# A decoder layer on one core: delta times h on GpSimd, the softmax's division behind the mix, six joins, the skip product by ScalarE, new queue orders

## The chip, the cores and the metric

One core of a Trainium2 chip runs the kernel. The time is the device time in microseconds of one execution, from the first instruction to the last. Only TensorE, VectorE (DVE in the profile), ScalarE (ACT), GpSimd (POOL) and the DMA queue that SyncE (SP) feeds take part.

## What is computed

128 sequences of 64 tokens with 128 features pass through one layer of three sublayers, each added to its input and followed by a layer norm: a Mamba block, a cross attention with 16 heads of 8, and a mixture of 8 experts (top 2) with a shared one. Cut to what the change touches:

```python
conv = silu(causal_conv4(hidden))                 # h in the kernel
delta = softplus(ts @ dt_w + dt_b)
new = exp(A * d_t) * state + d_t * B_t * h_t      # 16 states for each of 256 channels
y = einsum('bin,bn->bi', new, C_t) + D * h_t      # D * h is the skip product
out = (y * silu(gate)) @ out_w
...
scores = einsum('bhqd,bhkd->bhqk', qh, kh) / sqrt(8)
attn = softmax(scores)                            # exp and a division by the row's sum
out = einsum('bhqk,bhkd->bhqd', attn, vh) @ Wo.T + bo
```

## The kernel before, in words

The tokens are cut into 16 chunks of 8 sequences (T = 512 tokens), everything in fp32 but the B rows. A chunk passes through five stages: head (RMS norm, input projection), front (convolution, delta), scan (the 16 states), back (output of the block, attention, routing, the experts' first half) and tail (rest of the experts, last norm). In turn t, chunk t is in scan, t+1 in front, t+2 in head, t-1 in back and t-2 in tail, so up to five chunks are in flight. What each engine does in a turn, and in what order, is written out by hand as a list of steps for each of the four engines and SyncE, in three versions: FIRST_TEXT for the turns up to 1, ORDER_TEXT for the middle, LAST_TEXT from turn 15. An engine runs its list strictly in order and waits on semaphores; where the list begins a turn is only a cut in a cycle. Four PSUM banks form a ring (IN_RING) that TensorE's steps take in the order of its own list.

The steps that matter here:

- **delta** (VectorE, L1049) adds the two parts of the softplus; behind it in the same step VectorE multiplies delta with h into u (L1052), 128 x 1024. **drive** n (L1008) multiplies u with the B row, which TensorE has spread over the partitions (B_row, L609), into PSUM. **decay** (ScalarE, L766) is exp(A delta), one step per state and half. **scan** n (L1018) runs the recurrence over all tokens. **prod** n (GpSimd, L1149) multiplies the state with the C row, which SyncE has fetched (step C, L578) into one of four slots.
- **y_sum** (TensorE, L627) adds prod n into p_y through the identity matrix, one matmul for each of the two halves. For n in JOINED GpSimd first adds prod n-1 to prod n (L1154), and n-1 has no matmuls. **y_d** (L618) is the first matmul into p_y, diag(D) times h, and clears the bank. **gated** (VectorE, L1059) multiplies p_y with the gate.
- The attention of a chunk goes sequence by sequence, i = 0 to 7: **score** (TensorE, L697, with VectorE's row maximum, L1068), **exp** (ScalarE, L898, 8 activations that also give the sums den), **sum** (VectorE, L1072, reciprocal of den), **scale** (GpSimd, L1202, ex times the reciprocal), **turn** (TensorE, L702, four transposes, which wait for scale; ScalarE copies them out, L907), **mix** (TensorE, L710; copied out into aT, L913), and after four sequences **aout** (L716, L717), the output projection.
- **k** (GpSimd, L1193, L1196) and **km** (ScalarE, L887) build the masked keys from kT; **add_bo** is L1185. **x1T** is copied at L862 and the first convolution tap is L812. In the expert part **up_g** and **up_u** (TensorE, L728) feed ScalarE's tanh (L937) and copies (L945), VectorE (L1118, L1123) and GpSimd's gu and cw (L1214, L1223), which reads routing weights fetched by **cw_in** (L589).

```python
if i >= C_SLOTS or c.m >= 1:                               # step C, SyncE
    sp.wait_ge(prod_ready.sem, prod_ready.at(c.m, i - C_SLOTS))
...
pe.wait_ge(scale_ready.sem, scale_ready.at(c.m, i))        # step turn, TensorE
```

## Time and profile before

| | |
|---|---|
| median of 3 runs | 1906.67 us (1904.21 to 1908.64) |
| the profiled execution: its own time | 1910.89 us |
| its span, first to last instruction | 1909.1 us |
| mean granted TensorE clock | 0.962 of full |
| matmul records, TensorE | 7035 |
| DMA | 140.50 MB, 74 GB/s on average |

The page gives busy time per engine and groups the instructions by line. Further views cut the span into stretches, list who waited for whom, and follow the chain that ended last. An fp32 matmul shows as two matmul records. Mean durations of ScalarE and TensorE overlap with the next instruction's, so the pitch, where it matters, is read from a run of equal instructions.

### The profile page before, as it was taken

To read this page: it belongs to the slowest core of one execution; us is meant where nothing else is said; L and a number is where in the kernel's file an instruction comes from. 1 tells how busy PE (TensorE), PEld (TensorE's weight loads), DVE (VectorE), ACT (ScalarE), POOL (GpSimd) and SP (SyncE) were. 2 spreads that over 40 slices of the span, in tenths; PEclk is the share of its full clock that TensorE was granted. 3 is DMA by queue.
4 is the path that set the end of the run, shared out by engine and by line. 5 is a ranking of instruction groups with operands and counts; after the bars stand their busy time and mean duration, and the time that the engine had idled before them with its cause. 6 is when DMAs were issued, how large, how long until landed. Compare 5 with 4: busy or idle time off the path is not lost. (4 is left out here: it accounts for less than half of the span.)

```text
span 1909.1 us, 25699 instructions
## 1 busy us (share of the span) xinstructions
PE 1684.5 (88%) x7035; PEld 964.7 (51%) x7138; DVE 1539.7 (81%) x1891; ACT 1398.8 (73%) x4370; POOL 1529.5 (80%) x1284
## 2 busy tenths in 40 slices
PE   3679989999898999999899899989989999998976
PEld 1235454655545465554646455464645546465544
DVE  4988988888888888889888888888888888878422
ACT  5478787786977768787777869777787977867361
POOL 0578888888888888888888898888889888898734
PEclk7789999999999999999999999999999999999988
DMA  3212221313222131222213122221312222121102
GB/s 103 80 47 73 88 75 61 95 40 96 82 84 78 52 91 54 89 75 96 81 52 92 53 90 82 89 79 52 90 55 89 76 82 83 66 85 55 63 7 66
DMA packets 125918, 140.50 MB, mean 74 GB/s; under 512 B 44048, under 2 KB 69456, under 8 KB 125776
## 3 DMA queue, kind: packets, MB, share of 16 engines
q1 hardware_dynamic: 125776, 138.86, 23.8%
q8 instruction: 58, 0.95, 0.2%
q14 instruction: 84, 0.69, 0.1%
HBM read 133.84 MB, written 4.98 MB: 73 GB/s over the span
## 5 line engine op out<-in xcount | busy, mean ns | idle before, releaser
L1149 POOL TENSOR_TENSOR prod<-state,c_rep 128x1024 f32<-128x1024 f32 x256 | 605.4, 2368 | 39.8 <-PE p_y L627 23.7
L1018 DVE TENSOR_TENSOR_SCAN state<-decay,p_drive 128x1024 f32<-128x1024 f32 x256 | 584.6, 2284 | 28.5 <-ACT decay L766 15.2
L627 PE MATMUL p_y<-prod,ident 128*128 128x512 f32 x768 | 391.4, 609 | 10.2 <-POOL prod L1149 5.7
L766 ACT ACTIVATE decay<-delta,a_neg 128x504 f32<-128x504 f32 x512 | 359.3, 725 | 43.4 <-DVE state L1018 42.0
L1008 DVE TENSOR_TENSOR p_drive<-u,p_drive 128x1024 f32<-128x1024 f32 x256 | 312.2, 1220 | 66.4 <-PE p_drive L609 36.2
L898 ACT ACTIVATE ex<-p_ring,nmax 128x64 f32<-128x64 f32 x1024 | 310.1, 369 | 19.8 <-DVE nmax L1068 19.4
L898 ACT ACTIVATION_READ_ACCUMULATOR ex<-p_ring,nmax 128x1 f32 x1024 | 255.4, 262 | 0.0
L728 PE MATMUL p_ring<-x2T,wg 128*128 128x512 f32 x416 | 226.8, 650 | 13.2 <-ACT gh L823 12.3
L1202 POOL TENSOR_TENSOR ex<-ex,rden 128x512 f32<-128x512 f32 x128 | 144.2, 1127 | 94.1 <-DVE rden L1072 94.1
L728 PE MATMUL p_ring<-x2T,wu 128*128 128x512 f32 x416 | 208.9, 603 | 7.5 <-DVE km L1118 6.5
L627 PEld LDWEIGHTS p_y<-prod,ident 128*128 128x128 f32 x768 | 139.6, 194 | 143.8 <-issue 116.9
L1223 POOL TENSOR_TENSOR km<-km,cwr 128x512 f32<-128x512 f32 x128 | 179.6, 1413 | 21.5 <-DMA cwr<-cw_rows 20.3
L937 ACT ACTIVATE gt<-p_ring 128x512 f32<-128x512 f32 x208 | 123.0, 593 | 88.7 <-PE p_ring L728 88.1
L922 ACT ACTIVATE x<-p_ring,shift,rstd 128x128 f32<-128x128 f32 x192 | 78.2, 463 | 148.7 <-POOL shift L1174 147.9
L697 PE MATMUL p_ring<-km,qs 128*128 128x512 f32 x256 | 135.4, 622 | 25.6 <-ACT x L922 12.7
L1154 POOL TENSOR_TENSOR prod<-prod 128x1024 f32<-128x1024 f32 x64 | 151.6, 2368 | 5.0
L710 PE MATMUL p_ring<-exT,vm 128*128 128x128 f32 x1024 | 140.6, 280 | 10.1 <-ACT exT L907 8.3
L728 PEld LDWEIGHTS p_ring<-x2T,wg 128*128 128x128 f32 x416 | 82.3, 205 | 126.2 <-issue 82.9
L710 PEld LDWEIGHTS p_ring<-exT,vm 128*128 128x128 f32 x1024 | 125.0, 191 | 33.1 <-issue 12.0
L744 PE MATMUL p_ring<-wd,km 128*128 128x128 f32 x1024 | 127.9, 279 | 6.9 <-POOL acts_more L1223 6.8
L1214 POOL TENSOR_TENSOR km<-km,us 128x512 f32<-128x512 f32 x80 | 102.6, 1285 | 38.4 <-ACT us L945 37.0
L992 DVE BATCH_NORM_STATS2 stats<-p_ring 128x6 f32<-128x128 f32 x192 | 47.1, 287 | 105.4 <-PE p_ring L744 78.9
(139 smaller groups left out, 3080.1 us busy)
## 6 DMA issues: line engine op xcount, KB each, us to landing
c_rep<-c_rows SPq DMA_DIRECT2D x256, 256.0 KB, 3.6
cwr<-cw_rows SPq DMA_DIRECT2D x64, 256.0 KB, 3.2
ctxT<-in_ctx_t SPq DMA_DIRECT2D x32, 256.0 KB, 5.6
cwr<-cw_rows SPq DMA_DIRECT2D x32, 224.0 KB, 3.1
cwr<-cw_rows SPq DMA_DIRECT2D x32, 192.0 KB, 2.7
cwr<-cw_rows SPq DMA_DIRECT2D x32, 160.0 KB, 2.9
xf<-in_x SPq DMA_DIRECT2D x16, 256.0 KB, 5.9
xb<-in_x SPq DMA_DIRECT2D x16, 256.0 KB, 4.8
```

Source lines behind the costliest of these rows:

```text
L627: pe.matmul(p_y[1 - first][:], ident[:], prod[:, slot_of(c, n), 1 - first, :], start=False, stop=n == STATE - 1).then_inc(prod_used.sem, 1)
L697: mm = pe.matmul(p[:], qs[:, i, :, :].rearrange("p s q -> p (s q)"), km[:, i, :, :].rearrange("p a k -> p (a k)"), start=True, stop=True)
L710: mm = pe.matmul(p[:, 0:128], vm[:, i, q, :], exT[:, q, :], start=q == 0, stop=q == QUADS - 1)
L728: mm = pe.matmul(p[:], (wg if name == "up_g" else wu)[:, i, :], x2T[:], start=True, stop=True)
L766: act.activation(decay[:, n % 2, j, :].rearrange("p (b t) -> p b t", t=SEQ)[:, :, 1:], delta[:, c.parity, j, :].rearrange("p (b t) -> p b ...
L898: e = act.activation(ex[:, i % 2, a, :], p[:, a * SEQ:(a + 1) * SEQ], ACT.Exp, bias=nmax[:, i % 2, a:a + 1], accum_out=den[:, i % 2, a:a + 1])
L1008: dve.tensor_tensor(p_drive[:], u[:, c.parity, :, :], p_b.unsqueeze(1).to_broadcast([128, HALVES, T]), ALU.mult).then_inc(drive_ready.sem, 1)
L1018: dve.tensor_tensor_scan(state[:, slot_of(c, n), :, :].rearrange("p j t -> p (j t)"), decay[:, n % 2, :, :].rearrange("p j t -> p (j t)"), ...
L1149: pool.tensor_tensor(mine, state[:, slot_of(c, n), :, :], c_rep[:, n % C_SLOTS, :].unsqueeze(1).to_broadcast([128, HALVES, T]), ALU.mult). ...
L1154: pool.tensor_tensor(mine, mine, prod[:, slot_of(c, n - 1), :, :], ALU.add).then_inc(join_ready.sem, 1)
L1202: pool.tensor_tensor(ex[:, i % 2, :, :], ex[:, i % 2, :, :], by_group(rden[:, i % 2, :]).to_broadcast([128, PAIRS, SEQ]), ALU.mult).then_i ...
L1223: pool.tensor_tensor(acts[i], acts[i], cwr[:, slot, :], ALU.mult).then_inc(act_ready.sem, 1)
```

## The change

- JOINED has six members where it had four.
- The product u leaves VectorE's delta step and becomes a step of GpSimd, in the stage front. delta, drive0 and scan0 stand in front as well.
- The skip product: y_d is a step of ScalarE, which writes D times h straight into p_y; the matmuls of y_sum add to that. diag_d goes. Two matmuls at the start write p_y once.
- Softmax: scale goes; turn takes the undivided exponentials. sum takes the reciprocals of four sequences at once. ScalarE's new step spread repeats each reciprocal over the 8 features of its head, into kT's space; TensorE's new step rden transposes that by the identity into a bank of the ring; VectorE's new step share multiplies four sequences of aT by it. aout waits for share.
- All lists of steps are new. Shown are those of GpSimd and SyncE for the middle turns and the end of ScalarE's, which continues with scan.decay6 and back.v0; VectorE's list has "tail.up_g12 back.gated0 back.gated1". In it ScalarE's spread0 stands between decay19 and exp6, y_d1 between decay11 and q0, spread1 behind turn7.

```diff
--- before.py
+++ after.py
@@
-JOINED = (1, 9, 11, 13)
+SIDE = CHUNK_B // 2
+JOINED = (1, 3, 7, 9, 11, 13)
@@ ORDER_TEXT @@
     "act": (
...
+        "head.hid0 head.tap0 back.up_g11 front.gate_tanh1 back.up_g12 back.up_u10 front.decay4 "
+        "head.hid1 scan.k0 head.gate0 head.tap1 front.decay5 front.y_d0"),
...
     "pool": (
-        "tail.cw10 back.stats0 back.stats1 scan.prod0 tail.stats4 scan.prod1 back.k0 tail.stats5 "
-        "scan.prod2 back.scale0 scan.prod3 back.scale1 back.scale2 scan.prod4 scan.prod5 back.add_bo0 "
-        "back.scale3 scan.prod6 back.scale4 scan.prod7 scan.add_out_b0 back.scale5 scan.prod8 "
-        "back.scale6 back.stats2 back.scale7 scan.prod9 scan.prod10 back.stats3 scan.prod11 "
-        "scan.prod12 back.r_rank0 back.gu1 scan.prod13 back.cw0 back.cw1 back.gu2 head.mean0 back.gu4 "
-        "back.cw2 back.gu5 scan.prod14 back.cw3 back.cw4 scan.prod15 back.cw5 back.cw6 back.gu7 "
-        "back.gu8 back.cw7 back.cw8 back.gu10 back.cw9"),
+        "tail.cw7 tail.gu8 tail.cw8 tail.cw9 tail.gu10 tail.cw10 back.stats0 back.stats1 scan.prod0 "
+        "tail.stats4 scan.prod1 back.k0 tail.stats5 scan.prod2 scan.prod3 scan.prod4 scan.prod5 "
+        "back.add_bo0 scan.prod6 scan.prod7 scan.prod8 back.stats2 scan.prod9 scan.prod10 "
+        "scan.add_out_b0 back.stats3 scan.prod11 back.r_rank0 scan.prod12 back.gu1 scan.prod13 "
+        "back.gu2 back.cw0 head.mean0 back.cw1 front.u0 back.gu4 back.cw2 back.cw3 scan.prod14 "
+        "back.gu5 back.cw4 scan.prod15 back.cw5 back.gu7 back.cw6"),
     "sp": (
-        "back.C7 back.C10 scan.C_out0 back.C13 back.C11 back.C12 tail.cw_out0 tail.cw_in0 back.C14 "
-        "tail.cw_in1 back.C15 tail.cw_in2 tail.cw_in3 tail.cw_in4 scan.C0 tail.cw_in5 tail.cw_in6 "
-        "tail.cw_in7 scan.C1 scan.C3 tail.cw_in8 tail.cw_in9 tail.cw_in10 scan.C5 scan.C2 scan.C4 "
-        "scan.C6 scan.xb_in0 head.x_in0 tail.out0 scan.C9 scan.C8"),
+        "tail.cw_in5 scan.C2 tail.cw_in6 tail.cw_in7 tail.cw_in8 tail.cw_in9 scan.C3 tail.cw_in10 "
+        "scan.C5 scan.C4 scan.C9 scan.C7 scan.C8 scan.C6 scan.C11 head.x_in0 scan.C10 tail.out0 "
+        "scan.C13 front.C_out0 scan.xb_in0 scan.C12 front.C0 scan.C14 back.cw_out0 back.cw_in0 "
+        "back.cw_in1 back.cw_in2 scan.C15 back.cw_in3 front.C1 back.cw_in4"),
...
         ga = kT[:]
+        spread = kT[:].rearrange("p (b c) -> p b c", c=128)
...
             pe.matmul(p_b[:, 0:D], column(V_BV).to_broadcast([128, 128]), wattn[:, 3, :],
                       start=True, stop=True).then_inc(bv_ready.sem, 1)
+            for j in range(HALVES):
+                pe.matmul(p_y[j][:], ident[:], wattn[:].rearrange("d w o -> d (w o)"),
+                          start=True, stop=True).then_inc(y_open.sem, 1)
             def spread_b(c, n):
...
-            def skip_d(c, i):
-
-                j = 1 - i
-                pe.wait_ge(h_ready.sem, h_ready.at(c.m, j))
-                if c.m >= 1:
-                    pe.wait_ge(yg_ready.sem, yg_ready.at(c.m - 1, i))
-                pe.matmul(p_y[j][:], diag_d[:, j, :], h[:, c.parity, j, :], start=True, stop=False)
-
             def sum_n(c, k):
                 n, first = divmod(k, HALVES)
+                if sum_index(k) < HALVES:
+                    pe.wait_ge(skip_ready.sem, skip_ready.at(c.m, first))
                 if n in JOINED:
                     pe.wait_ge(join_ready.sem, join_ready.at(c.m, JOINED.index(n)))
                 else:
                     pe.wait_ge(prod_ready.sem, prod_ready.at(c.m, n))
                 pe.matmul(p_y[1 - first][:], ident[:], prod[:, slot_of(c, n), 1 - first, :],
-                          start=False, stop=n == STATE - 1).then_inc(prod_used.sem, 1)
+                          start=False, stop=n == STATE - 1, skip_group_check=True
+                          ).then_inc(prod_used.sem, 1)
             def step(name, i, c):
                 if name == "less":
...
                 elif name == "turn":
-                    pe.wait_ge(scale_ready.sem, scale_ready.at(c.m, i))
+                    emptied(pe, "score", i, c.m)
                     for q in range(QUADS):
                         mm = pe.transpose(p[:, q * 128:(q + 1) * 128],
...
+                elif name == "rden":
+                    pe.wait_ge(spread_ready.sem, spread_ready.at(c.m, i))
+                    for b in range(SIDE):
+                        mm = pe.matmul(p[:, b * 128:(b + 1) * 128], spread[:, b, :], ident[:], start=True, stop=True)
                 elif name == "aout":
                     pe.wait_ge(x1b_ready.sem, x1b_ready.at(c.m))
-                    emptied(pe, "mix", (i + 1) * CHUNK_B // 2 - 1, c.m)
+                    emptied(pe, "rden", i, c.m)
                     for g in range(2):
                         pe.matmul(p[:, g * D:(g + 1) * D], ident[:], x1b[:, 2 * i + g, :], start=True, stop=False)
                         mm = pe.matmul(p[:, g * D:(g + 1) * D],
...
                     act.wait_ge(max_ready.sem, max_ready.at(c.m, i))
+                    if c.m >= 1:
+                        act.wait_ge(rden_ready.sem, rden_ready.at(c.m - 1, i // SIDE))
                     for a in range(PAIRS):
                         e = act.activation(ex[:, i % 2, a, :], p[:, a * SEQ:(a + 1) * SEQ], ACT.Exp,
-                                           bias=nmax[:, i % 2, a:a + 1], accum_out=den[:, i % 2, a:a + 1])
+                                           bias=nmax[:, i % 2, a:a + 1], accum_out=den[:, i, a:a + 1])
                     e.then_inc(free("score", i, c.m), 1)
                 elif name == "turn":
                     p = filled(act, name, i, c.m)
@@ -906,6 +906,18 @@
                         filled(act, "mix", CHUNK_B - 1, c.m - 1)
                     act.activation(exT[:].rearrange("p a q -> p (a q)"), p[:],
                                    ACT.Copy).then_inc(free(name, i, c.m), 1)
+                elif name == "spread":
+                    act.wait_ge(rden_ready.sem, rden_ready.at(c.m, i))
+                    if i == 0:
+                        act.wait_ge(km_ready.sem, km_ready.at(c.m))
+                        act.wait_ge(km_more.sem, km_more.at(c.m))
+                    else:
+                        filled(act, "rden", 0, c.m)
+                    mine = rden[:, SIDE * i:SIDE * (i + 1), :].unsqueeze(3).to_broadcast([128, SIDE, PAIRS, HEAD_D])
+                    for s in range(2):
+                        a = act.activation(spread[:, :, 64 * s:64 * s + 64].rearrange("p b (a d) -> p b a d", d=HEAD_D),
+                                           mine, ACT.Copy)
+                    a.then_inc(spread_ready.sem, 1)
                 elif name == "mix":
                     p = filled(act, name, i, c.m)
                     for s in range(2):
...
                 elif name == "decay":
                     decays(c, i)
+                elif name == "y_d":
+                    j = 1 - i
+                    act.wait_ge(h_ready.sem, h_ready.at(c.m, j))
+                    if c.m >= 1:
+                        act.wait_ge(yg_ready.sem, yg_ready.at(c.m - 1, i))
+                    else:
+                        act.wait_ge(y_open.sem, y_open.at(0, j))
+                    act.activation(p_y[j][:], h[:, par, j, :], ACT.Copy, scale=column(V_D + j)
+                                   ).then_inc(skip_ready.sem, 1)
...
                     dve.tensor_tensor(delta[:, par, :, :], delta[:, par, :, :], sp_a[:], ALU.add
                                       ).then_inc(delta_ready.sem, 1)
-                    dve.wait_ge(delta_ready.sem, delta_ready.at(c.m))
-                    dve.tensor_tensor(u[:, par, :, :], delta[:, par, :, :], h[:, par, :, :], ALU.mult
-                                      ).then_inc(u_ready.sem, 1)
                 elif name == "gated":
                     j = 1 - i
...
                 elif name == "sum":
-                    emptied(dve, "score", i, c.m)
-                    dve.reciprocal(rden[:, i % 2, :], den[:, i % 2, :]).then_inc(rden_ready.sem, 1)
+                    mine = slice(SIDE * i, SIDE * i + SIDE)
+                    emptied(dve, "score", SIDE * i + SIDE - 1, c.m)
+                    if c.m >= 1:
+                        dve.wait_ge(spread_ready.sem, spread_ready.at(c.m - 1, i))
+                    dve.reciprocal(rden[:, mine, :].rearrange("p b a -> p (b a)"),
+                                   den[:, mine, :].rearrange("p b a -> p (b a)")).then_inc(rden_ready.sem, 1)
+                elif name == "share":
+                    p = filled(dve, "rden", i, c.m)
+                    emptied(dve, "mix", SIDE * i + SIDE - 1, c.m)
+                    mine = slice(SIDE * SEQ * i, SIDE * SEQ * (i + 1))
+                    for s in range(2):
+                        r = slice(64 * s, 64 * s + 64)
+                        a3 = aT[r, mine].rearrange("p (b q) -> p b q", q=SEQ)
+                        d = dve.tensor_tensor(a3, a3, p[r, :].rearrange("p (b s q) -> p b s q", b=SIDE, s=2)[:, :, s, :],
+                                              ALU.mult)
+                    d.then_inc(free("rden", i, c.m), 1)
                 elif name == "route":
                     p = filled(dve, name, i, c.m)
                     logits = p[:, 0:GROUPS * EXPERTS].rearrange("p (g e) -> p g e", e=EXPERTS)
...
                                                masks[:, a:a + 1], 0.0, ALU.mult, ALU.add)
                     g.then_inc(km_ready.sem, 1)
-                elif name == "scale":
-                    emptied(pool, "score", i, c.m)
-                    pool.wait_ge(rden_ready.sem, rden_ready.at(c.m, i))
-                    pool.tensor_tensor(ex[:, i % 2, :, :], ex[:, i % 2, :, :],
-                                       by_group(rden[:, i % 2, :]).to_broadcast([128, PAIRS, SEQ]),
-                                       ALU.mult).then_inc(scale_ready.sem, 1)
                 elif name == "r_rank":
                     pool.wait_ge(route_v.sem, route_v.at(c.m, 4))
                     pool.tensor_tensor(r_eq, r_eq, tri[:].unsqueeze(1).to_broadcast(
                         [128, GROUPS, EXPERTS, EXPERTS]), ALU.mult).then_inc(route_g.sem, 1)
                     pool.wait_ge(route_g.sem, route_g.at(c.m, 0))
                     pool.tensor_tensor(r_gt, r_gt, r_eq, ALU.add).then_inc(route_g.sem, 1)
+                elif name == "u":
+                    pool.wait_ge(h_ready.sem, h_ready.at(c.m, 1))
+                    pool.wait_ge(delta_ready.sem, delta_ready.at(c.m))
```

## Rows read from the trace of the kernel before

**Rows 1.** The page: busy time, share and instructions of each engine
```profile
PE 1684.5 (88%) x7035; PEld 964.7 (51%) x7138; DVE 1539.7 (81%) x1891; ACT 1398.8 (73%) x4370; POOL 1529.5 (80%) x1284
```

**Rows 2.** The delta step: shortest, median, longest in ns, first and last start
```profile
L1049 DVE TENSOR_TENSOR delta<-delta,sp_a x16: 1224/1271/1972, 40.2 to 1662.4; 128x1024 f32<-128x1024 f32 x16
```

**Rows 3.** Busy time by stretch: the lead-in and ten periods
```profile
core 0: us, PE busy (x) PEld busy (x) DVE busy (x) ACT busy (x) POOL busy (x), PEclk, DMA share, GB/s
0.00:208.45 208.45, 141.48 (x394) 63.40 (x400) 161.10 (x164) 137.76 (x361) 118.07 (x80) 0.83 0.23 70
...
321.04:1437.65 1116.61, 1024.65 (x4388) 593.43 (x4459) 960.60 (x1170) 869.21 (x2731) 957.85 (x801) 0.99 0.25 77
```

**Rows 4.** The chain that ended last, in time: start, us, what
```profile
1775.68 4.29 PE p_ring L728 x10
...
1800.70 2.90 PE p_ring L744 x26
```

**Rows 5.** Groups of TensorE: busy and mean | idle before
```profile
L627 PE MATMUL p_y<-prod,ident 128*128 128x512 f32 x768 | 391.4, 609 | 10.2 <-POOL prod L1149 5.7 <-POOL prod L1154 4.3
...
L618 PE MATMUL p_y<-h,diag_d 128*128 128x512 f32 x64 | 32.4, 621 | 0.1
```

**Rows 6.** Groups of GpSimd
```profile
L1149 POOL TENSOR_TENSOR prod<-state,c_rep 128x1024 f32<-128x1024 f32 x256 | 605.4, 2368 | 39.8 <-PE p_y L627 23.7 <-DVE state L1018 11.9 <-DMA c_rep<-c_rows 4.2
...
L1202 POOL TENSOR_TENSOR ex<-ex,rden 128x512 f32<-128x512 f32 x128 | 144.2, 1127 | 94.1 <-DVE rden L1072 94.1
```

**Rows 7.** Waits in ten periods, 321.04 to 1437.65: us, times, longest
```profile
POOL ex L1202 <- DVE rden L1072: 54.0, 40, 2.3
...
PE p_ring L702 <- POOL ex L1202: 5.3, 20, 0.3
```

**Rows 8.** VectorE: u's shortest, median, longest in ns, then groups
```profile
L1052 DVE TENSOR_TENSOR u<-delta,h x16: 1225/2170/2178, 41.4 to 1663.7; 128x1024 f32<-128x1024 f32 x16
...
L1123 DVE TENSOR_TENSOR km<-kT,p_ring 128x512 f32<-128x512 f32 x48 | 32.5, 677 | 1.6 <-PE p_ring L728 1.2
...
L1052 DVE TENSOR_TENSOR u<-delta,h 128x1024 f32<-128x1024 f32 x16 | 31.9, 1994 | 0.6
L1072 DVE RECIPROCAL rden<-den 128x8 f32<-128x8 f32 x128 | 24.4, 191 | 9.7 <-ACT ex L898 9.7
...
L1091 DVE TENSOR_TENSOR x1T<-r_prob 128x256 f32<-128x256 f32 x16 | 6.8, 424 | 0.6
```

**Rows 9.** Groups of ScalarE
```profile
L937 ACT ACTIVATE gt<-p_ring 128x512 f32<-128x512 f32 x208 | 123.0, 593 | 88.7 <-PE p_ring L728 88.1 <-DVE km L1118 0.4
...
L913 ACT ACTIVATE aT<-p_ring 64x64 f32<-64x64 f32 x256 | 58.0, 226 | 8.3 <-PE p_ring L710 6.6
L887 ACT ACTIVATE km<-kT,masks 128x512 f32<-128x512 f32 x48 | 31.1, 712 | 29.8 <-PE p_ring L744 29.8
...
L812 ACT ACTIVATE zc<-hpad,halfv 128x512 f32<-128x512 f32 x32 | 25.8, 807 | 0.1
...
L862 ACT ACTIVATE x1T<-p_ring 128x256 f32<-128x256 f32 x32 | 11.9, 380 | 1.6 <-PE p_ring L678 1.6
```

**Rows 10.** Busy time by stretch: the attention part of one period
```profile
820.50:838.50 18.00, 15.93 (x59) 8.20 (x60) 16.67 (x19) 17.88 (x96) 15.42 (x10) 1.00 0.43 110
```

**Rows 11.** The C rows: issue ns, waits, landing us, and add_bo
```profile
L578 SPq DMA_DIRECT2D c_rep<-c_rows x256: 319/426/1450, 30.9 to 1763.8; - x128
...
  DMA c_rep<-c_rows: 4.2, 1
...
DMA to landing us min/median/max: 3.0/3.6/6.1
...
L1185 POOL TENSOR_TENSOR x1b<-x,rowb 128x512 f32<-128x512 f32 x16 | 20.4, 1274 | 0.0
```

**Rows 12.** VectorE in order of time: two successive scans
```profile
831.46 2.29 DVE L1018 TENSOR_TENSOR_SCAN state<-decay,p_drive 128x1024 f32<-128x1024 f32 x1
...
836.02 2.29 DVE L1018 TENSOR_TENSOR_SCAN state<-decay,p_drive 128x1024 f32<-128x1024 f32 x1
```

62 lines of the change are left out of this document (48 added, 14 removed), and 260 rows, old and new, of tables (FIRST_TEXT, LAST_TEXT, ORDER_TEXT).

## The prediction

> **What bounds the kernel now.** I read the page's first part, then cut the span at the delta step, which comes once per chunk, then the waits, and last the long groups of each engine. The page names TensorE the busiest engine [rows 1]. There are 16 delta steps, the last at 1662.4 us [rows 2]; the third is at 208.45, so 13 periods take 1454.0 us, 111.8 us for one chunk. In ten whole periods from 321.04 to 1437.65 TensorE is busy for 1024.65 of 1116.61 us, VectorE for 960.60, GpSimd for 957.85 and ScalarE for 869.21 [rows 3]. Per period that is TensorE 102.5 busy and 9.2 idle, VectorE 96.1, GpSimd 95.8, ScalarE 86.9. The granted clock there is 0.99, the 2.4 GHz level, so there is nothing to win from the clock in the middle. What is idle on TensorE is split into many short gaps, and in long runs of 512-column matmuls there is no gap at all. I therefore take TensorE's instruction stream as the bound, with VectorE and GpSimd 6 us behind. The reader should see in [rows 1] how close the four engines stand: whatever is taken from TensorE alone pays in full only until the next one is full.
>
> **TensorE, part by part.** An fp32 matmul is two records. Ten records of 512 columns take 4.29 us, so one such matmul costs 0.86 us; 26 records of 128 columns take 2.90 us, so a small one costs 0.223 [rows 4]. Two more joins drop two states from the sum into p_y, each with two matmuls: 4 x 0.86 = 3.44 us less per chunk. The skip product leaves TensorE: 64 records in 16 chunks are 2 matmuls per chunk [rows 5], 1.72 us less. The new step rden has 2 x 4 fp32 matmuls of 128 columns: 8 x 0.223 = 1.78 us more. Net: **3.4 us less per chunk**. The two matmuls that open p_y run once, during the load; if nothing hid them they would cost 2 x 1.7 us at most, twice 0.86, as the clock's mean in the lead-in is 0.83 [rows 3] and part of it is at the lower level, and I take zero.
>
> **GpSimd.** Eight scale steps go: 144.2 us in 16 chunks, 9.0 per chunk, and with them the 94.1 us that GpSimd stood waiting for VectorE's reciprocal [rows 6], 5.9 per chunk. Two joins come, 2 x 2.37 = 4.7 us, and u, a 1024-wide product of two SBUF tiles like prod, 2.37 us [rows 6]. Net busy time **1.9 us less**, and one in-order wait less: every product behind a scale used to wait for an exp, a reciprocal and two semaphores.
>
> On VectorE, u takes 1.99 us on average, but its shortest is 1.23 and its median 2.17 [rows 8]: I read this as an operation held up beside GpSimd's own two-input work, so the move costs GpSimd little more than VectorE gives back. The Trainium skill, GPSIMD Engine Reference, section 4.1 Engine selection, speaks against the move: elementwise work belongs on VectorE, as two-input operations are about 2x slower on GpSimd. By the shortest VectorE time this trace agrees (2.37 against 1.23), by the median it doesn't; by the page the move would hand 1.1 us more to GpSimd than it frees, by the rows 0.2 to 0.4, and in neither case does GpSimd end above today.
>
> **VectorE.** Gone: u 1.99 and eight reciprocals, 8 x 0.19 = 1.53 [rows 8]. New: two reciprocals of 32 columns; bounds 0.19 (8 columns) and 0.42 (256 columns), I take 0.2 each, nearer in size to the first. New too: four products share, 64 partitions x 256 columns, one input in PSUM; bounds 0.19 and the 0.68 of a 512-column product from PSUM; I take 0.42, the 256-column product [rows 8]. Net 3.52 - 0.4 - 1.68 = **1.4 us less**, between +0.04 more and 2.4 less by the bounds.
>
> **ScalarE.** Two y_d steps, 512 columns with a scale, written to PSUM. No row shows a ScalarE write to PSUM; the nearest are the scaled copy from SBUF, 0.71 us, and copies of the same width at 0.59; the upper end is 0.81 for the first tap. I take 0.71. Four spread steps of 128 x 256: 0.38 as in x1T, between 0.23 (64 x 64) and 0.71 [rows 9]. Sum 1.42 + 1.54 = **3.0 us more** (2.1 to 4.5). ScalarE has 24.8 us idle per period, which hides most of it, but from 820.5 to 838.5 us it is busy for 17.88 of 18.00 us [rows 10]. That is the exp part. spread0 now stands in it, y_d1 before it, y_d0 and spread1 well outside; I charge spread0's two instructions, 0.76 us, and hide the rest. y_d0 ends ScalarE's turn and waits for gated0 of the chunk before; decay6 and the copies of v stand behind it. gated0 comes right after VectorE's up_g12 step, two instructions of 0.68 us behind the tanh that they wait for [rows 8], and after that tanh ScalarE has seven more steps of 504 or 512 columns, 0.59 to 0.81 us each [rows 9]; so I take no stall there.
>
> **The softmax chain.** A transpose now waits for the exp only; 0.19 and 1.05 us and two hand-overs leave each of eight chains. TensorE waited directly for scale for only 5.3 us in ten periods [rows 7], so I book at most 0.5 per chunk, and take 0. In their place aout waits for mix, rden and share: 8 small matmuls and 2 x 0.42, under 3 us twice per chunk. TensorE has other steps queued there, turn5 or x2T; I take 0.
>
> **The sum.** 3.44 + 1.72 - 1.78 - 0.76 = 2.62 us per chunk. It holds in 13 periods, and once more for the lead-in and the last scan together: in the first 208 us TensorE is busy for 141 only [rows 3]. After the last scan, the attention of the last chunk runs alone; there the scale goes from the chain and share comes into it, which I set equal. 14 x 2.62 = 36.7 us. The profiled execution took 1910.9 us around a span of 1909.1; it becomes 1874.2, and from the median of 1906.67, which stands 4.2 below it, 1870.0. **Forecast 1870 us.** The new orders are assumed to bring the work into place and no more.
>
> **The rivals.**
>
> **More than the sum (0.17).** GpSimd is the second bound, and loses 1.9 busy and up to 5.4 of waiting per period (54.0 us in ten periods [rows 7]), 7.3 in all. If the period goes half by TensorE and half by GpSimd, it shrinks by (3.4 + 7.3) / 2 = 5.3 us: 14 x 5.3 = 75, time 1832. For it: GpSimd feeds both p_y and the expert part. Against it: these waits let state_ready come up anyway, since the products follow the scans.
>
> **ScalarE eats it (0.12).** If all the 3.0 us stand in the full stretch, the period loses only 0.4: 1901. At the bounds of its price the period goes from 1.3 us less to 1.1 more, 1888 to 1922. For it: the full stretch in [rows 10]. Against it: y_d0 and spread1 lie outside it, and the queue's order can move decays.
>
> **Slower: a late C row (0.10).** The order of SyncE's queue now has C9, C7, C8, C6. C9 waits for prod5, and C6, which prod6 reads, is queued behind it. After prod5 ends there are four issues of 0.43 us and 3.6 to land, 5.3 us, and only add_bo's 1.28 us lies between prod5 and prod6 [rows 11]: GpSimd idles for 4.0 us. It decides from the point where scan6 ends earlier than 4.0 us after add_bo could start prod6, and where GpSimd, not TensorE, sets the period; the scans are 111.8 / 16 = 7.0 us apart on average, though 4.6 in places [rows 12], so most of it hides behind VectorE. If nothing hid, 4.0 against the 3.4 saved: 14 x 0.6 = 8 slower, 1915; with ScalarE's 0.8, 1926. Against it: today's C7 is queued behind C9 in the same way, and all waits of the products for c_rep come to 4.2 us [rows 11].
>
> **It doesn't do what it says (0.04).** If the order of the queues, not the work, sets the period, and the search had won nothing, the time stays within 0.2%, 1903 to 1910.
>
> **How the numbers follow.** The forecast's own case has 0.57 and spans 1852 to 1891: the ends are ScalarE charged at 0 with the 0.5 of the softmax chain (14 x 3.9 = 55) and ScalarE at 2.3 of its 3.0. For 8 in 10 I reach down to 1838, over part of the first rival, and up to 1904, over the second; the slower case and the lower end of the first are left out. A difference under 0.2% can't be told from none in this kernel. Faster by more than that: 0.57 + 0.17 + 0.09 of the second rival = 0.83; within: 0.04 + 0.02 = 0.06; slower: 0.10 + 0.01 = 0.11.
>
> **What would show it.** In the changed profile: the sum into p_y with 640 records at the same 0.86 pitch and no matmul of h; GpSimd's busy time down by some 30 us over the span and its wait for rden gone; VectorE's u gone and the share group near 0.42 us; ScalarE's busy time up by some 48 us; delta steps 109.2 us apart; TensorE's idle time per period still about 9 us or a little more. I am wrong if that idle time grows by more than 2 us, and the releaser then says why: ScalarE's exT or gt for the second rival, c_rep in front of prod for the third. If TensorE's idle time falls as well, the first rival holds. A GpSimd wait for delta in front of u, or VectorE's drive0 waiting for u, would be a cost that I left out.

## The result, and the profile after

The changed kernel takes 1921.38 us (median of 6 runs, 1912.70 to 1931.27), the kernel before 1907.30 on the same chip (6 runs, 1904.21 to 1910.05). The ratio is **1.0071 (95% interval 1.005 to 1.0091)**: slower by 0.7%, where 1870 was forecast, and outside the forecast's range. The profiled execution took 1921.7 us around a span of 1919.6, against 1910.9 and 1909.1, so the spans show 10.5 of the 13.5 us.

The page after, its first part and the groups that answer to [rows 1, 5, 6] (busy time, mean ns | idle before, by releaser):

```profile
PE 1664.9 (87%) x7206; PEld 964.4 (50%) x7206; DVE 1540.6 (80%) x1841; ACT 1448.2 (75%) x4466; POOL 1515.8 (79%) x1204
...
L1178 POOL TENSOR_TENSOR prod<-state,c_rep 128x1024 f32<-128x1024 f32 x256 | 611.1, 2395 | 163.7 <-PE p_y L622 80.3
...
L622 PE MATMUL p_y<-prod,ident 128*128 128x512 f32 x640 | 343.4, 633 | 13.4 <-POOL prod L1183 12.0
...
L1183 POOL TENSOR_TENSOR prod<-prod 128x1024 f32<-128x1024 f32 x96 | 230.0, 2396 | 7.5
```

The edit did what it says: 640 records in the sum, no matmul of h, no scale step. TensorE is busy for 19.6 us less although its clock was lower, ScalarE for 49.4 more, GpSimd for 13.7 less. But GpSimd now stands idle for 163.7 us in front of prod, where it was 39.8 [rows 6]: in place of the 94 us that it no longer waits for VectorE's reciprocal stand 124 us more of other waits, in front of prod alone.

The delta step after, as in [rows 2], and the stretches that answer to [rows 3], with the one behind the last delta:

```profile
L1067 DVE TENSOR_TENSOR delta<-delta,sp_a x16: 1226/1876/1890, 39.2 to 1665.3; 128x1024 f32<-128x1024 f32 x16
```
```profile
0.00:210.35 210.35, 136.66 (x401) 62.58 (x401) 157.47 (x159) 143.33 (x372) 124.94 (x79) 0.81 0.25 74
320.80:1440.57 1119.77, 1017.21 (x4501) 593.59 (x4500) 963.59 (x1141) 900.84 (x2791) 950.30 (x751) 0.97 0.26 76
1665.29:1919.60 254.31, 209.60 (x961) 131.90 (x960) 129.80 (x202) 137.50 (x473) 157.33 (x152) 0.92 0.19 57
```

The third delta starts at 210.35, the last at 1665.29: 13 periods of 111.9 us, where they were 111.8 and 109.2 was forecast. So the middle gained nothing (+1.0 us in all), the lead-in took 1.9 us more, and what follows the last delta 254.3 instead of 246.7, 7.6 more. In the ten periods TensorE is idle for 10.3 us each (9.2 before), and its **granted clock is 0.97** where it was 0.99.

Where that clock is lost, in slices of 4 us inside one period after (columns as in [rows 3]; the clock is the third number from the end):

```profile
818.00:822.00 4.00, 1.46 (x4) 0.63 (x5) 3.49 (x6) 3.96 (x10) 2.72 (x8) 0.97 0.00 0
822.00:826.00 4.00, 3.58 (x5) 0.79 (x3) 1.07 (x2) 3.97 (x20) 4.00 (x2) 0.60 0.00 0
866.00:870.00 4.00, 2.54 (x13) 1.74 (x14) 2.94 (x5) 3.16 (x8) 3.92 (x3) 0.94 0.00 0
870.00:874.00 4.00, 4.00 (x6) 1.13 (x5) 3.27 (x8) 1.52 (x3) 2.30 (x3) 0.63 0.00 0
```

Twice in the period the clock is at the 1.2 GHz level for most of a slice, each time behind a slice in which TensorE did little. Only the first place is new: behind x2T the clock of the kernel before falls too, in most of its periods (0.57 from 757 to 761 us). The first place before, then the order in time of what TensorE did there before and after (start, us, what, and the idle time in front):

```profile
818.00:822.00 4.00, 2.70 (x7) 0.75 (x6) 3.49 (x3) 3.94 (x14) 3.84 (x7) 1.00 0.00 0
822.00:826.00 4.00, 3.97 (x10) 1.46 (x8) 3.60 (x7) 4.00 (x26) 1.70 (x3) 1.00 0.34 89
```
```profile
814.95 1.06 PE L690 MATMUL p_ring<-wattn,ctxT 128*128 128x128 f32 x8
816.06 1.02 PE L681 MATMUL p_ring<-x1T,wattn 128*128 128x512 f32 x2
816.92 1.88 PE L618 MATMUL p_y<-h,diag_d 128*128 128x512 f32 x4
819.25 1.10 PE L697 MATMUL p_ring<-km,qs 128*128 128x512 f32 x2 [0.45 <-ACT qs L866]
```
```profile
816.78 1.05 PE L684 MATMUL p_ring<-wattn,ctxT 128*128 128x128 f32 x8
819.79 0.39 PE L610 MATMUL p_drive<-xp,sel_bc 128*128 128x512 bf16 x1 [1.95 <-DVE state L1036]
820.92 1.23 PE L691 MATMUL p_ring<-km,qs 128*128 128x512 f32 x2 [0.74 <-ACT km L885]
821.95 1.91 PE L622 MATMUL p_y<-prod,ident 128*128 128x512 f32 x2
823.78 1.79 PE L691 MATMUL p_ring<-km,qs 128*128 128x512 f32 x2
```

Before, the skip product (L618) ran in this place while ScalarE prepared the queries and keys. After, nothing stands there, TensorE is idle for 1.95 and 0.74 us, and the matmuls that follow start 1.83 us apart (821.95 to 823.78) in place of 0.86: the half clock. The second place, at 867, lies around x2T, behind a wait of 1.16 us for the norm.

What such a drop costs can be read inside one execution, without any change to the kernel. Of the ten periods of the kernel before, seven show a clock of 0.98 and last 112.1 us on average, three show 1.00 and last 110.6. Two neighbours:

```profile
657.78:770.32 112.54, 103.06 (x439) 59.57 (x446) 96.23 (x118) 86.94 (x274) 95.69 (x81) 0.98 0.25 76
770.32:881.12 110.80, 100.80 (x437) 58.72 (x445) 95.79 (x118) 86.92 (x274) 95.47 (x81) 1.00 0.25 77
```

In the changed kernel eight of the ten are at 0.97 and last 112.5 us, the two at 0.98 last 109.7 and 110.1 (VectorE is some 3 us less busy in these two, so not all of that is the clock).

Waits in the ten periods after (us in total, times, longest), and GpSimd in order of time where it waits longest:

```profile
PEld p_drive L610 <- DVE state L1036: 70.6, 89, 2.1
...
POOL prod L1178 <- PE p_y L622: 48.3, 17, 4.6
...
POOL prod L1178 <- issue: 44.2, 12, 4.6
```
```profile
837.38 1.27 POOL L1214 TENSOR_TENSOR x1b<-x,rowb 128x512 f32<-128x512 f32 x1
843.07 2.35 POOL L1178 TENSOR_TENSOR prod<-state,c_rep 128x1024 f32<-128x1024 f32 x1 [4.42 <-issue]
```

The second fence is the late C row of the slower rival: prod6 starts 4.42 us after add_bo ends, where 4.0 was worked out. There were thus two candidates for the lost time: the **clock theory** (gaps left on TensorE put it on the lower level twice per period) and the **C row theory** (GpSimd's 4.4 us per period set the pace).

### The profile page after: what moved, and what is told of

It is laid out like the page before. It is cut to its first block and busy times, and to the rows that moved or that the text cites. A ratio compares the mean times of both kernels' runs of the same rounds, so it can differ in the third digit from the quotient of the medians.

```text
span 1919.6 us, 26072 instructions
## 1 busy us (share of the span) xinstructions
PE 1664.9 (87%) x7206; PEld 964.4 (50%) x7206; DVE 1540.6 (80%) x1841; ACT 1448.2 (75%) x4466; POOL 1515.8 (79%) x1204
## 5 line engine op out<-in xcount | busy, mean ns | idle before, releaser
L1178 POOL TENSOR_TENSOR prod<-state,c_rep 128x1024 f32<-128x1024 f32 x256 | 611.1, 2395 | 163.7 <-PE p_y L622 80.3
L622 PE MATMUL p_y<-prod,ident 128*128 128x512 f32 x640 | 343.4, 633 | 13.4 <-POOL prod L1183 12.0
L898 ACT ACTIVATION_READ_ACCUMULATOR ex<-p_ring,nmax 128x1 f32 x1024 | 248.1, 248 | 0.0
L1183 POOL TENSOR_TENSOR prod<-prod 128x1024 f32<-128x1024 f32 x96 | 230.0, 2396 | 7.5
L622 PEld LDWEIGHTS p_y<-prod,ident 128*128 128x128 f32 x640 | 118.1, 200 | 138.0 <-issue 94.6
L1253 POOL TENSOR_TENSOR km<-km,cwr 128x512 f32<-128x512 f32 x128 | 166.3, 1305 | 20.8 <-DMA cwr<-cw_rows 20.8
L691 PE MATMUL p_ring<-km,qs 128*128 128x512 f32 x256 | 151.3, 678 | 19.1 <-ACT km L885 8.2
L610 PE MATMUL p_drive<-xp,sel_bc 128*128 128x512 bf16 x256 | 101.7, 397 | 75.6 <-DVE state L1036 75.6
L1083 DVE TENSOR_REDUCE nmax<-p_ring 128x8 f32<-128x512 f32 x128 | 87.4, 683 | 73.6 <-PE p_ring L691 72.9
L726 PEld LDWEIGHTS p_ring<-x2T,wu 128*128 128x128 f32 x416 | 76.3, 192 | 109.9 <-issue 76.5
L1244 POOL TENSOR_TENSOR km<-km,us 128x512 f32<-128x512 f32 x80 | 114.7, 1437 | 16.4 <-ACT us L957 16.4
```

The lines of the kernel that those rows point to most:

```text
L622: pe.matmul(p_y[1 - first][:], ident[:], prod[:, slot_of(c, n), 1 - first, :], start=False, stop=n == STATE - 1, skip_group_check=True).th ...
L691: mm = pe.matmul(p[:], qs[:, i, :, :].rearrange("p s q -> p (s q)"), km[:, i, :, :].rearrange("p a k -> p (a k)"), start=True, stop=True)
L726: mm = pe.matmul(p[:], (wg if name == "up_g" else wu)[:, i, :], x2T[:], start=True, stop=True)
L898: e = act.activation(ex[:, i % 2, a, :], p[:, a * SEQ:(a + 1) * SEQ], ACT.Exp, bias=nmax[:, i % 2, a:a + 1], accum_out=den[:, i, a:a + 1])
L1178: pool.tensor_tensor(mine, state[:, slot_of(c, n), :, :], c_rep[:, n % C_SLOTS, :].unsqueeze(1).to_broadcast([128, HALVES, T]), ALU.mult). ...
L1183: pool.tensor_tensor(mine, mine, prod[:, slot_of(c, n - 1), :, :], ALU.add).then_inc(join_ready.sem, 1)
```

## The experiments

"Period" is the mean distance of the delta steps, from the third to the last, of the profiled execution; for the changed kernel it is 111.9 us, where the expectations write 112.4. Ratios are to the kernel before on the same chip, with the 95% interval.

### Three probes of the two theories

**c_rising** fetches C2 to C15 in the order of their numbers (C13 comes behind xb_in by that):

```diff
-        "scan.C5 scan.C4 scan.C9 scan.C7 scan.C8 scan.C6 scan.C11 head.x_in0 scan.C10 ..."
+        "scan.C4 scan.C5 scan.C6 scan.C7 scan.C8 scan.C9 scan.C10 head.x_in0 scan.C11 ..."
```

> The changed kernel, but the C rows of a chunk are fetched in rising order (C6, C7, C8, C9 and so on), in the same places of SyncE's list. If the late C6 row holds the kernel back (GpSimd idles 4.4 us in front of prod6 in each period, twelve such waits in ten periods), the period of 112.4 us falls by 2 to 4 us and the time from 1921 to about 1870 to 1890. If the granted clock or TensorE's own order sets the period, GpSimd's wait goes, another wait takes its place, and the time stays within 5 us of 1921.

**warm** adds useless work on TensorE ahead of both gaps, writing the same values a second and third time: 8 more matmuls of 128 columns in v1 and one more of 512 columns in dt0, 2.64 us per chunk by the pitches of [rows 4].

```diff
-                    mm = pe.matmul(p[:], wdt[:, i * 128:(i + 1) * 128], xp_sb[0:RANK, :], start=True, stop=True)
+                    for again in range(2 - i):
+                        mm = pe.matmul(p[:], wdt[:, i * 128:(i + 1) * 128], xp_sb[0:RANK, :], start=True, stop=True)
...
-                    for b in range(4):
+                    for b in range(4 * (1 + 2 * i)):      # b % 4 inside
```

> The changed kernel with more work on TensorE: the matmuls of v1 three times and that of dt0 twice, with the same operands and the same result, in the two places where TensorE idles in front of the two stretches at half the clock (822 to 826 and 870 to 874 us in one period). Work added: 1.8 + 0.9 us per chunk. Theory clock: the two stretches at half the clock give back the 3.4 us of matmuls that the change saved; with the gaps filled they go, the granted clock from 320 to 1440 us rises from 0.97 to 1.0, the period falls to 109.5 to 111 us and the time to 1880 to 1900, although TensorE has more to do. Theory order: the clock rises or not, but the period stays at 112.4 or grows by up to 2.7 us: 1921 to 1960.

**warm_rising** makes both edits.

> Both edits together: C rows in rising order and the repeated matmuls. If the two costs are independent, the gains of the two single kernels add. If only one of them sets the period, the time is that of the better single kernel.

| kernel | us | ratio | period |
|---|---|---|---|
| c_rising | 1928.7 | 1.0095 (1.0068 to 1.0122) | 112.5 |
| warm | 1903.97 | 0.9969 (0.9956 to 0.9981) | 109.9 |
| warm_rising | 1923.78 | 1.0068 (1.0049 to 1.0088) | 111.7 |

The C row theory misses: prod's wait for a row ("issue") is gone in c_rising, yet the kernel is not faster (0.2% slower by the ratios, with intervals that overlap). GpSimd's wait for p_y takes its place, over the whole span (80.3 us in the changed kernel):

```profile
POOL prod L1034 <- PE p_y L478: 130.2, 37, 9.9
```

The clock theory hits: with 2.6 us **more** work per chunk warm is 1% faster than the change. The period of 109.9 is as expected, the time of 1904 lies 4 us above the expected range. Its clock over ten periods is full:

```profile
320.00:1420.00 1100.00, 1020.84 (x4685) 608.00 (x4684) 948.69 (x1141) 900.41 (x2793) 952.93 (x751) 1.00 0.27 78
```

warm_rising misses: it was to be as fast as warm and is 1% slower, about as slow as the change, although its clock from 320 to 1460 us is 0.99. Against warm, fetching the C rows in order thus costs time by itself, and a nearly full clock alone does not make the kernel fast. Why is taken up under warm_c6.

### The two gaps apart

**warm_v** has the extra matmuls of v1 alone, **warm_dt** that of dt0 alone, **warm_mid** both, but only in chunks 2 to 13.

> The changed kernel with v1's matmuls three times (1.8 us more per chunk, in front of the first stretch at half the clock), dt0 once. Theory clock: the first of the two stretches goes, the second stays; half of the gain of the run warm or a little more, 1907 to 1918. Theory order: 1921 or above.

> The changed kernel with dt0's matmul twice (0.9 us more per chunk, in front of the second stretch at half the clock), v1 once. Theory clock: the second stretch goes, the first stays; 1907 to 1920. Theory order: 1921 or above.

> The run warm, but with the repeated matmuls for chunks 2 to 13 only. In the run warm the lead-in up to the third delta grew from 210.4 to 213.8 us, where filling can't help. Expected 3 us off: 1900 to 1902, below the kernel before by 0.4 to 0.6%.

Measured: 1907.46, ratio 1.0 (0.9983 to 1.0017); 1908.17, ratio 0.9999 (0.9983 to 1.0015); 1900.96, ratio 0.9967 (0.9956 to 0.9979), period 110.3. By the ratios, either gap filled gives about 14 us against the change, both about 20. To fill them in the first and last chunks too, as in warm, brings nothing. All three lie in their expected ranges.

### Each part alone, in the orders of before

Here the code of one part is changed, and its steps are put into the old lists where the steps that they replace stood, or behind what they wait for. **all_old** has all four parts.

```diff
-        JOINED = (1, 9, 11, 13)                     # joins: two matmul steps of each new pair leave
+        JOINED = (1, 3, 7, 9, 11, 13)
+        "... back.score7 back.rden0 ... back.mix7 back.rden1"    # divide, TensorE
+        "... back.mix3 back.spread0 ... back.turn7 back.spread1" # divide, ScalarE
+        "... front.u0 head.mean0"                   # u_pool, GpSimd
+        "... scan.decay11 scan.y_d0 scan.y_d1"      # yd_act, ScalarE
```

> The kernel before with six joins instead of four, nothing else; its orders without y_sum4, 5, 12 and 13. TensorE has 3.4 us less per chunk, GpSimd 4.7 us more (95.8 to 100.5 of 111.8). If TensorE's work sets the period, 1865 to 1880. If GpSimd or the waits between them do, 1915 to 1980; with GpSimd's 4.7 in full on the path, 14 x 4.7 = 66, 1973.

> The kernel before with the softmax's division behind the mix, nothing else; the new steps are put in its lists as in the run all_old. GpSimd has 9.0 us less work and 5.9 less waiting per chunk, ScalarE 1.5 more in its full stretch, TensorE 1.8 more. If GpSimd's waits behind VectorE's reciprocals hold the kernel back, 1860 to 1890. If ScalarE and TensorE set the attention part, plus 1.5 to 3.3 per chunk: 1925 to 1955.

> The kernel before with u on GpSimd (in front of mean0), nothing else. GpSimd has 2.4 us more, VectorE 2.0 less per chunk. With both 6 us below TensorE: no change, 1900 to 1915. If drive0 waits for u behind GpSimd's queue: 1920 to 1945.

> The kernel before with the skip product written to PSUM by ScalarE behind decay11, nothing else. TensorE has 1.7 us less, ScalarE 1.4 more, right in front of its full stretch. If TensorE's work sets the period: 1885 to 1895. If the full stretch of ScalarE does: 1915 to 1930. If the 1.7 us that TensorE no longer works in front of the scores drop its granted clock, as the theory of the run warm has it, 1905 to 1925 with a mean clock from 320 to 1440 us below today's 0.99.

> All four parts of the change (six joins, u on GpSimd, skip product by ScalarE, division behind the mix) in the orders of the kernel before: removed steps are taken out of its lists and the new ones are put in at the nearest place (y_d0 and y_d1 behind decay11, u in front of mean0, sum0 and sum1 where sum3 and sum7 stood, spread0 behind mix3, rden0 and share0 behind score7, spread1 behind turn7, rden1 behind mix7, share1 in front of stats3). If the parts save what the work says and the new orders lose it, 1870 to 1895. If the parts themselves cost it (joins that make GpSimd wait for TensorE, more on ScalarE in its full stretch), 1905 to 1940.

| kernel | us | ratio |
|---|---|---|
| joins | 1951.29 | 1.0207 (1.0162 to 1.0252) |
| divide | 2030.53 | 1.0616 (1.0594 to 1.0638) |
| u_pool | 1933.1 | 1.0105 (1.0082 to 1.0128) |
| yd_act | 1938.4 | 1.0138 (1.0115 to 1.0161) |
| all_old | 2048.86 | 1.0724 (1.0684 to 1.0765) |

Each part alone costs time, 23 to 120 us; all together 138, less than their sum of 212. So no part is a gain at the places that it was given here: orders that fit are part of the price. joins and u_pool lie in the ranges of their slower cases; divide, yd_act and all_old are slower than anything that was expected of them. The largest, divide, over 320 to 1500 us: busy time, then waits (its period is 119.6):

```profile
320.00:1500.00 1180.00, 1041.22 (x4480) 621.76 (x4549) 970.42 (x1139) 879.53 (x2747) 870.89 (x712) 0.97 0.24 72
```
```profile
POOL prod L1035 <- DVE state L890: 54.1, 21, 3.4
...
PE p_drive L463 <- DVE state L890: 37.0, 20, 3.0
...
DVE aT L956 <- PE p_ring L569: 17.1, 10, 2.3
```

GpSimd is busy for only 74% of this stretch. The products and TensorE's B rows wait for VectorE's scans, and VectorE itself waits in front of share for TensorE's rden. How much of this is my choice of the places and how much the part itself wasn't separated.

**yd_both** asks whether yd_act loses by the clock. TensorE keeps its two matmuls in the old places (they only open p_y), and ScalarE writes D times h over them. A second thing differs from yd_act: ScalarE's two steps stand behind q0, not in front of it, and wait for those matmuls.

```diff
+                    pe.matmul(p_y[1 - i][:], ident[:], wattn[:].rearrange("d w o -> d (w o)"),
+                              start=True, stop=True).then_inc(y_open.sem, 1)
...
+                    act.wait_ge(y_open.sem, y_open.at(c.m, i))
```

> The kernel before with the skip product by ScalarE as in yd_act, but TensorE keeps two matmuls into p_y at the same places (identity times the attention weights; ScalarE then writes D times h over them, behind q0). TensorE's work and its places are those of the kernel before. Theory clock: the 28 us that yd_act lost come mostly from the 1.7 us that TensorE no longer worked in front of the scores; they come back, 1908 to 1920, with the granted clock near 0.99 again. Theory ScalarE: the two writes in front of its full stretch cost the time, 1930 to 1945.

Measured 1944.14, ratio 1.0194 (1.0176 to 1.0212), period 114.2: in the range of the ScalarE theory, and slower than yd_act (1.0138, period 113.8). It doesn't acquit the clock, though. The stretch from 320 to 1460 us in yd_act and in yd_both, then TensorE in yd_act in front of the scores:

```profile
320.00:1460.00 1140.00, 1032.29 (x4369) 594.20 (x4428) 963.54 (x1173) 885.59 (x2754) 959.40 (x802) 0.97 0.25 75
320.00:1460.00 1140.00, 1046.89 (x4462) 597.68 (x4461) 961.22 (x1171) 880.72 (x2751) 952.43 (x802) 0.98 0.25 75
```
```profile
830.55 1.79 PE L546 MATMUL p_ring<-km,qs 128*128 128x512 f32 x2 [3.34 <-ACT qs L715]
```

In yd_act ScalarE's writes delay q0, TensorE stands 3.3 us per period waiting for the queries, and the scores behind that run at the half clock: the step on ScalarE and the missing work on TensorE make the gap together. In yd_both this wait is back at 0.4 us, but the clock only at 0.98, not at 0.99. What its 114.2 us consist of wasn't separated.

### The skip product back on TensorE, in the new orders

**skip_pe** takes the change as it is and undoes one part. **skip_pe_dt** also computes dt0 twice, for the second gap, in chunks 2 to 14. **before_dt** does the latter to the kernel before.

```diff
-        ... front.decay5 front.y_d0"  /  "... scan.decay11 scan.y_d1 back.q0 ..."  # ScalarE
+        "... back.v1 scan.y_d0 scan.y_d1 ..."                                      # TensorE
+                pe.matmul(p_y[j][:], diag_d[:, j, :], h[:, c.parity, j, :], start=True, stop=False)
```

> The changed kernel with the skip product back on TensorE (y_d0 and y_d1 behind v1 in the middle turns, behind q0 in the first and last ones; ScalarE's y_d goes). TensorE has 1.7 us more per chunk, in the gap in front of the first stretch at half the clock, ScalarE 1.4 less. Theory clock: like warm_v, or better by what ScalarE saves: 1895 to 1908. By the work alone, as in my prediction, it would be 14 x 1.7 = 24 us slower than the changed kernel, 1945.

> As skip_pe, and dt0's matmul twice for chunks 2 to 14. Both stretches at half the clock go: 1888 to 1900, the fastest of all. By the work alone 1945 + 11.

> The kernel before with dt0's matmul twice for chunks 2 to 14 and nothing else: 0.9 us more work on TensorE per chunk. In one period shown of it, TensorE drops to half its clock at 757 us, behind the short gaps around x2T1. Theory clock: fewer such stretches, 1900 to 1908. By the work alone: 11 us slower, 1919.

| kernel | us | ratio | period |
|---|---|---|---|
| skip_pe | 1895.98 | 0.9937 (0.9912 to 0.9961) | 110.9 |
| skip_pe_dt | 1890.46 | 0.9911 (0.9893 to 0.9929) | 109.6 |
| before_dt | 1899.73 | 0.9957 (0.994 to 0.9974) | 111.1 |

The stretch of ten periods in skip_pe_dt, then in before_dt:

```profile
320.00:1420.00 1100.00, 1020.30 (x4568) 595.38 (x4567) 952.84 (x1144) 889.12 (x2784) 953.86 (x754) 1.00 0.27 78
```
```profile
320.00:1420.00 1100.00, 1023.47 (x4459) 590.48 (x4459) 948.26 (x1160) 858.53 (x2719) 947.62 (x797) 1.00 0.26 77
```

Against the change, 1.72 us more real work on TensorE per chunk, and 1.4 less on ScalarE, make the kernel 1.3% faster (0.9937 / 1.0071), and 0.86 us of useless work another 0.3%, though the two intervals overlap. Even the kernel before gains 0.4% from that one useless matmul: its clock of 0.99 [rows 3] was not free of such drops. skip_pe_dt beats both kernels, and all three lie within 1 us of their expected ranges.

Two pairs of runs tell TensorE's gap and ScalarE's step apart. warm_v fills the first gap and leaves y_d on ScalarE, skip_pe fills it with the skip product itself: 1.0 against 0.9937. warm_mid and skip_pe_dt are such a pair with both gaps filled: 0.9967 against 0.9911. In each pair TensorE's work differs by less than 0.1 us in nearly every chunk, and the intervals lie apart. So of the 25 us between the change and skip_pe about 14 come with the filled gap and some 11 with the step taken off ScalarE.

### Both waits away at once

**warm_c6** is warm_mid with one reordering, the narrow form of c_rising:

```diff
-        "scan.C5 scan.C4 scan.C9 scan.C7 scan.C8 scan.C6 scan.C11 ..."
+        "scan.C5 scan.C4 scan.C6 scan.C7 scan.C8 scan.C9 scan.C11 ..."
```

> The run warm_mid (1901), with C9, C7, C8, C6 of the middle turns changed to C6, C7, C8, C9 and nothing else of SyncE's order. If GpSimd's wait for the late C6 row costs the kernel its 3.5 us per period, 1860 to 1880. If other waits take its place, as most of it hides: 1896 to 1906.

Measured 1918.21, ratio 1.004 (1.0025 to 1.0056), period 111.3: 17 us slower than warm_mid, a miss. Waits over 320 to 1430 us, in warm_mid and then in warm_c6:

```profile
POOL prod L1179 <- issue: 40.0, 11, 4.7
POOL prod L1179 <- PE p_y L622: 33.4, 10, 3.9
...
POOL var L1197 <- DVE mv L1015: 22.8, 26, 1.3
```
```profile
POOL prod L1131 <- PE p_y L574: 68.6, 20, 3.9
...
POOL var L1149 <- DVE mv L967: 40.7, 24, 2.9
```

The wait for the row is gone, and 35.2 and 17.9 us come back for p_y and for VectorE's statistics. The C row's delay was one of several things that hold GpSimd back to the pace of the others. The clock is 1.00 in both, so it isn't the clock. What did get longer is a step of VectorE, h<-h,zc (the end of the convolution's silu), over the same stretch in warm_mid and in warm_c6:

```profile
L1060 DVE SCALAR_TENSOR_TENSOR h<-h,zc 128x512 f32<-128x512 f32 x20 | 13.6, 680 | 0.0
L1012 DVE SCALAR_TENSOR_TENSOR h<-h,zc 128x512 f32<-128x512 f32 x20 | 32.2, 1610 | 0.0
```

With the wait, GpSimd is idle while VectorE runs the second of the chunk's two such steps; without it, prod6 runs beside that step, which takes 2.4 to 2.9 us in place of 0.68. That is 1.9 us more per period for VectorE, where the period grew by 1.0. c_rising and warm_rising show the same (means of 1.45 and 1.47 us over the whole span, 0.70 in the changed kernel). It fits the slower times, but no run changed this alone.

## Why the prediction was wrong

**TensorE's work.** The terms were right in kind: 640 records, no y_d, the rden matmuls. At its own clock TensorE is busy 101.7 us per period against 102.5, with the lower clock inside it, so not the whole 3.4 shows. Where the clock is 1.00 on both sides the sum fits better: from before_dt to skip_pe_dt the joins and rden take 1.66 us off TensorE, and the period is 1.5 shorter (111.1, 109.6), though the other parts differ between these two as well.

**The step that failed** is "there is nothing to win from the clock in the middle", and with it pricing removed work at the pitch of busy TensorE and crediting it in full. There was nothing to win, but something to lose. The skip product's 1.72 us stood in a gap between the projections and the first scores. Taking it away saved nothing there, as the scores wait for ScalarE and VectorE anyway, and left 2.7 us of idle time, after which the clock was at 1.2 GHz. An estimate from the rows: a mean clock of 0.97 over 1119.8 us is 67 us at the lower level, 6.7 per period; the matmuls there started 1.83 us apart in place of 0.86, so it costs up to 3.4 us per period; with 0.99, before, up to 1.1. The means are rounded, so the difference lies between 1.1 and 3.4 us per period, and 2.62 is what I had booked as gained. With both gaps filled the period is 109.9 (warm) and, with the skip product in its place, 109.6 (skip_pe_dt), where 109.2 was forecast. A rule of the Trainium skill bears on it, in TensorE: Matmul & The Clock Gate, section A second HAM failure mode: psum-queue depth-cycling: short idles between groups of matmuls can make the clock swing between its two levels. By that rule, this trace agrees (1.00 to 0.60 behind 1.95 and 0.74 us of idle time). I hadn't asked of any removed operation whether it was what kept TensorE busy. My own sign of being wrong, more than 2 us of added idle time per period, didn't show it either: idle time grew by 1.1, since a TensorE at the half clock counts as busy.

This step doesn't carry the whole miss. Of the 51 us between forecast and result, filling the first gap gives back 14 and filling both 20; with the skip product back on TensorE as well it is 31 (skip_pe_dt), of which 8 were open to the kernel before, too (before_dt). For the other 20 no run names a cause.

**ScalarE eats it.** This rival was right in part. ScalarE's busy time grew by 3.2 us per period, near the 3.0 that I took, and I hid the two y_d steps (0.68 us each) because they lie outside the full stretch. They aren't free there: with TensorE's gap filled in both cases, the kernel with y_d on ScalarE is some 11 us slower than the one without (warm_v and skip_pe, warm_mid and skip_pe_dt). Which wait carries these 11 us wasn't followed. That the rival's upper end, 1922, is the measured time is chance: for 3.0 us it gave 1901.

**GpSimd.** 13.7 us less busy where 30 were expected; prod and join take 2.395 us each now, 2.368 before [rows 6], and 352 times 27 ns are 9.5 us of the difference. The 5.9 us of waiting per chunk did go, and came back as waits for p_y and for the C row, so the second bound gave nothing. The rival "more than the sum" needed it to. Its wait for delta in front of u, 31.0 us, is two waits, one of 29.8 in the lead-in, where it waited 32.2 for ScalarE before.

**The late C row.** Place and size were right (4.42 us against 4.0), and "slower" came true by luck, as the mechanism is not the cause: without the wait the kernel is no faster (c_rising, warm_rising, warm_c6). In that wait GpSimd left VectorE alone.

**VectorE.** Its busy time is 1540.6 us against 1539.7, where 22 less were forecast. The groups of the new pieces after, and of two old ones:

```profile
L1099 DVE TENSOR_TENSOR aT<-aT,p_ring 64x256 f32<-64x256 f32 x64 | 26.4, 413 | 15.5 <-PE p_ring L709 12.1 <-ACT aT L925 3.0
L918 ACT ACTIVATE kT<-rden 128x256 f32<-128x256 f32 x64 | 22.8, 406 | 0.2
...
L972 ACT ACTIVATE p_y<-h,vecs 128x512 f32<-128x512 f32 x32 | 21.7, 679 | 0.0
L1090 DVE RECIPROCAL rden<-den 128x32 f32<-128x32 f32 x32 | 10.9, 340 | 1.7 <-ACT ex L898 1.7
...
L1067 DVE TENSOR_TENSOR delta<-delta,sp_a 128x1024 f32<-128x1024 f32 x16 | 28.9, 1805 | 24.0 <-ACT sp_a L852 24.0
L1063 DVE SCALAR_TENSOR_TENSOR gate<-gate,gh 128x512 f32<-128x512 f32 x32 | 55.9, 1746 | 0.0
```

share, spread and y_d came at 0.41, 0.41 and 0.68 where 0.42, 0.38 and 0.71 were taken; only the reciprocal was far too small, 0.2 against 0.34. New against removed pieces give 26.4 + 10.9 - 31.9 - 24.4 = -19.0 us. Most of the gain was lost on others: delta took 21.3 us before and takes 28.9, the convolution's taps 101.4 and 108.6, 14.8 us more together; the last 5 us aren't assigned. What these operations of two SBUF inputs take goes with what GpSimd does beside them. In the changed kernel 29 of the 32 h steps ran with GpSimd idle and took 0.68 to 0.69 us, while the 16 gate steps of the same form that lay wholly beside its work took 0.85 to 2.71. Before, it was the other way round: 12 gate steps with GpSimd idle, 0.68 each, and 14 h steps beside its work, 1.28 to 2.30.

**The orders.** "The new orders are assumed to bring the work into place and no more" was a term set to zero. all_old against the change says that, with the four parts in the code, they are worth some 125 us against the places that I chose in the old lists. That the old lists fit the old steps so closely that a step moved alone opens waits is how I read the single parts; other places weren't tried.

**The end.** I set the tail of the last chunk equal. From the last chunk's first exp to the output projection's second half it took 32.6 us (1822.9 to 1855.5) against 30.1 before (1813.1 to 1843.2). The chain ahead of aout1:

```profile
1844.77 0.72 ACT kT L918 x2
...
1851.97 0.89 PE p_ring L709 x8
...
1854.21 0.23 ACT aT L925
1854.53 0.41 DVE aT L1099
1854.96 0.44 DVE aT L1099
```

Spread, rden and share stand in it, 2.5 us together, and that part of the end grew by 2.5. More was lost ahead of it: from the last delta to the last chunk's first exp it takes 157.6 us against 150.7, and what follows the projection is 1.7 us shorter, which gives the 7.6. In skip_pe and skip_pe_dt, which have the skip product back, the part ahead is 153.8 and 154.2 us, the part with the chain 32.6 as in the change. So setting the chain equal was wrong by 2.5 us, and the larger part of the loss lies ahead of the last chunk's attention. Neither was undone alone in a run, and the 1.9 us of the lead-in aren't assigned.

**Still open:** whether VectorE's longer step is what makes warm_c6 slower, what the last 20 us of the miss are, and why the parts one by one lose more than all of them together.

## What to carry to other kernels

Before crediting work taken off the busiest engine, look at what stands next to it in time: if it fills a gap that a wait would leave, it is worth nothing there, and on TensorE its removal can cost more than it weighed, by the granted clock of what follows. Read that clock in slices of a few microseconds and compare the periods of one execution with and without a drop, rather than trust a mean over periods: 0.99 and 0.97 look alike and are 1.1 to 3.4 us per period apart here. In a hand-written cyclic order, a single wait, even one whose length was forecast to 0.4 us, isn't a price until a run without it says so: an idle GpSimd can be what lets VectorE run at its short times.

## What the runs showed of the hardware

- Drops of TensorE's clock cost some 1.5 us per period here: periods of one execution of the kernel before last 112.1 us with a clock of 0.98 and 110.6 with 1.00.
- Useless matmuls pay: 2.6 us per chunk of them took the change from 1.0071 to 0.9969 of the kernel before, and 0.86 us in 13 chunks took the kernel before to 0.9957.
- A scaled copy of 512 columns by ScalarE from SBUF into PSUM averages 0.68 us; the scaled copy from SBUF took 0.71 [rows 9]. The Trainium skill, ScalarE: Activation LUTs, section Step-by-step: what each stage is for, says that PSUM is the quicker destination for ScalarE; the two rows agree, by 0.03 us, which is little for means that overlap with the next instruction.
- Operations of one kind differ by a factor of 2.5 on VectorE, with what GpSimd runs beside them. The gate's step, 128x512, took 0.70 us on average before (22.5 us in all) and 1.75 after; h's, of the same form and size, went the other way, 1.76 to 0.70, and in warm_c6, where only four C rows change places, from 0.68 to 1.61. A duration read from one order is not a price in another.
